# A split operand 64 bytes further, modulo 512, from the matrix it is mixed with

## The reference

```python
x = layernorm(x + attention(x))      # 16 heads, 4 key/value heads, old keys pooled in blocks of 64
x = layernorm(x + ffn(x))

def ffn(x):                          # x: [4096, 512]
    x = fwht(x * SU_ug) / 64         # Walsh-Hadamard transform over 512
    up   = x @ W_up.T   * (Wscale_ug[:2048] * 64)
    gate = x @ W_gate.T * (Wscale_ug[2048:] * 64)
    x = silu(gate) * up              # [4096, 2048]
    x = fwht(x * SU_dp) / 64         # over 2048
    return x @ W_down.T * (Wscale_dp * 64)
```

## Time and profile before

| | us |
|---|---|
| median of three runs | 1549.19 (1547.73 to 1554.15) |
| the profiled execution | 1548.87 |
| its span in the profile | 1547.1 |
| TensorE busy | 1513.5 |
| VectorE busy | 1034.0 |
| ScalarE busy | 625.8 |
| GpSimd busy | 465.0 |

### The profile page before, as it was taken

The page is one execution under the profiler, slowest core; times in us unless marked ns, Lnnn a source line. Parts: engine busy times, 40 slices in busy tenths (PEclk is TensorE's granted clock), DMA queues, the critical chain, the costliest instruction groups (busy, mean ns, idle before and its releaser), DMA issues.

```text
span 1547.1 us, 29636 instructions
## 1 busy us (share of the span) xinstructions
PE 1513.5 (98%) x11744; PEld 1422.1 (92%) x11744; DVE 1034.0 (67%) x1790; ACT 625.8 (40%) x1289; POOL 465.0 (30%) x580
## 2 busy tenths in 40 slices
PE   6999999999999999999999999999999999999998
PEld 5977978888887899899999999999999999999998
DVE  6876787677687886865575576566467547557645
ACT  4263245236227755533333343343343333334332
POOL 5465457438338533500220030030040022003001
PEclk9999999999999999999999999999999999999999
DMA  7031122122112796678578667767776857866862
GB/s 284 1 116 69 35 83 102 35 82 103 64 64 101 275 378 246 236 273 307 205 242 295 231 241 263 268 216 264 272 238 226 322 195 257 288 231 231 283 234 97
DMA packets 92072, 307.63 MB, mean 199 GB/s; under 512 B 9888, under 2 KB 10272, under 8 KB 90144
## 3 DMA queue, kind: packets, MB, share of 16 engines
q1 hardware_dynamic: 90928, 301.54, 54.8%
q10 hardware_dynamic: 1008, 4.20, 0.7%
HBM read 255.37 MB, written 50.33 MB: 198 GB/s over the span
## 4 chain that ended last, share of the span: by engine, by line
PE 64%; DVE 4%; ACT 1%; issue 1%; POOL 1%; POOLq 0%; DVEq 0%; ACTq 0%
PE ff_bank_b L2061 16%; PE ff_bank_a L2061 11%; PE ff_bank_c L2061 11%; PE ff_acc L2095 8%; PE ff_acc L2098 7%; PE ff_acc L2086 7%; DVE ff_d_lo L1775 2%; PE ff_x_ps L2020 1%; PE ff_x_ps L2009 1%; PE ff_x_ps L2032 1%; ACT at_union L601 1%; DVE ff_c L1826 0%; DVE ff_h_lo L1794 0%; DVE ff_c L1822 0%; DVE ff_ring L1770 0%
## 5 line engine op out<-in xcount | busy, mean ns | idle before, releaser
L2061 PE MATMUL ff_bank_b<-ff_x_hi,ff_ring 128*128 128x256 f32 x1536 | 296.8, 278 | 4.1 <-DVE ff_c L1826 3.5
L2061 PEld LDWEIGHTS ff_bank_b<-ff_x_hi,ff_ring 128*128 128x128 f32 x1536 | 246.3, 188 | 5.6 <-issue 5.4
L2061 PE MATMUL ff_bank_b<-ff_x_lo,ff_ring 128*128 128x256 f32 x768 | 212.8, 277 | 0.0
L2095 PE MATMUL ff_acc<-ff_d_lo,ff_h_hi 128*128 128x256 f32 x1008 | 199.8, 279 | 2.4 <-DVE ff_d_lo L1775 2.4
L2061 PE MATMUL ff_bank_c<-ff_x_hi,ff_ring 128*128 128x256 f32 x1024 | 200.3, 280 | 0.0
L2061 PE MATMUL ff_bank_a<-ff_x_hi,ff_ring 128*128 128x256 f32 x1024 | 199.6, 279 | 0.0
L2098 PE MATMUL ff_acc<-ff_d_hi,ff_h_lo 128*128 128x256 f32 x1008 | 197.7, 277 | 0.0
L2061 PEld LDWEIGHTS ff_bank_c<-ff_x_hi,ff_ring 128*128 128x128 f32 x1024 | 164.2, 188 | 2.2 <-issue 2.2
L2061 PEld LDWEIGHTS ff_bank_a<-ff_x_hi,ff_ring 128*128 128x128 f32 x1024 | 164.3, 188 | 0.3 <-issue 0.2
L1822 DVE TENSOR_TENSOR ff_c<-ff_bank_b,ff_c 128x512 f32<-128x512 f32 x64 | 44.3, 692 | 172.0 <-PE ff_bank_b L2061 171.1
L2095 PEld LDWEIGHTS ff_acc<-ff_d_lo,ff_h_hi 128*128 128x128 f32 x1008 | 152.9, 188 | 6.4 <-issue 6.4
(11 more groups left out here) (321 smaller groups left out, 3482.3 us busy)
## 6 DMA issues: line engine op xcount, KB each, us to landing
ff_ring<-gu_scratch SPq DMA_DIRECT2D x392, 512.0 KB, 5.1
gu_scratch<-ff_ring SPq DMA_DIRECT2D x56, 512.0 KB, 4.3
at_xt<-in_xt SPq DMA_DIRECT2D x4, 2048.0 KB, 8.0
at_xn<-in_x SPq DMA_DIRECT2D x32, 256.0 KB, 2.9
x_scratch<-at_x SPq DMA_DIRECT2D x32, 256.0 KB, 2.0
ff_raw<-in_wgu SPq DMA_DIRECT2D x8, 1024.0 KB, 7.1
at_wd_a<-in_wd SPq DMA_DIRECT2D x8, 512.0 KB, 4.0
mixed_scratch<-at_wd_a SPq DMA_DIRECT2D x8, 512.0 KB, 3.3
```

What stands on the lines that cost most here:

```text
L2061: i = pe.matmul(bank[:, m, :], r[:, a, m, c, :], b[:, k, c, :], start=(k < 3 and m == 0 and c == 0 and b is x_hi and a == 0), stop=(m == 1 ...
L2095: pe.matmul(acc[:, t, half], h_hi[q][:, j, k], d_lo[:, j, half], start=False, stop=False, skip_group_check=True)
```

## The change

`gap_behind` grows by 16 floats, which is 64 bytes per partition, and a tile of 112 floats (448 bytes) is put behind the two split tiles. `xs_hi` and `xs_lo` then stand at 64 modulo 512; everything behind them moves by 512 bytes. No instruction changes but for these addresses.

```diff
         sb("gap_in_front", [P, 16])
         d_hi, d_lo = sb("d_hi", [P, 2, D], F32R), sb("d_lo", [P, 2, D], F32R)
         x_hi, x_lo = sb("x_hi", [P, MULS, 2, HB2], F32R), sb("x_lo", [P, MULS, 2, HB2], F32R)
-        sb("gap_behind", [P, 1008])
+        sb("gap_behind", [P, 1024])
         xs_hi, xs_lo = sb("xs_hi", [P, FB], F32R), sb("xs_lo", [P, FB], F32R)
+        sb("gap_after", [P, 112])
         xm = sb("xm", [P, 8, FB])
```

## The result

The changed kernel takes 1568.73 us, the median of four runs (1567.53 to 1570.90). The kernel before took 1551.67 in its four (1547.73 to 1554.52). The ratio is 1.0113, with a 95% interval of 1.0083 to 1.0143. The profiled execution of after is 1569.43, its span 1567.6. The ratios are taken from the single executions and are not the quotients of the medians, from which they differ by up to 0.0022. One execution of the kernel before, 1573.59 us at a granted clock of 0.947, is left out of every ratio and counts only in the median of 1554.90 of its session.

A forecast was written before the change was run, and what follows sets the result against it. TensorE's stream of 256-column matmuls, at two lasting paces, was taken as the bound. 1548.87 - 0.2 + 0.95 + 0.35 + 19.3 = 1569.3 us, 1569.5 against the median; range 1547.5 to 1572.

The forecast's parts named there:

- The mixing no longer restores: At every mixing (L2020): at offset 64 it leaves the pace as it finds it, always slow; groups behind stay 1.41 us.
- The mixing itself: The 112 mixing matmuls: each between 113.3 and 120.8 ns instead of about 118.5; -0.6 to +0.3 us, taken as -0.2.
- Stretches behind a mixing: Stretches made fast by a mixing turn slow: 0.95 us over six blocks, 0.35 us in the first two blocks.
- The wait gives back 0.48 us: Block-end wait on VectorE's eviction: absorbs the slower 108 matmuls ahead of it, cost 0; otherwise 2.9 us in all.
- The restarts come out slow: Behind the six block-end waits: entered slow, the stream stays slow; 14.3 us for five blocks, 5.0 behind the sixth.
- four slow restarts: First block of the earlier trace: four of five different restarts came out slow, taken as evidence for slow late restarts.
- rival of fast restarts: Block-end waits entered slow come out fast, the instant being set by VectorE and GpSimd: 1550.0 us, chance 0.27.
- the offset does nothing: Something else in the mixing switches the pace, so it goes on as before: 1549 us, chance 0.11.
- The mixture: Two to four blocks restart slow by chance of the instant: 1556 to 1562 us, chance 0.15.
- it restores always: Every mixing at the new offset restores the fast pace, making the kernel faster: 1543.7 us, chance 0.05.

The follow-up runs named there:

- hi_only: Kernel before with only xs_hi at 64 bytes modulo 512, xs_lo staying at 0, the rest as in the changed kernel: 1567.30 us, ratio 1.0102.
- lo_only: Kernel before with only xs_lo at 64 bytes modulo 512, xs_hi staying at 0: 1565.53 us, ratio 1.0091.
- late_m7: Changed kernel with a 64-column VectorE memset ahead of the eviction L1827 in the last pair of every block but the first: 1563.01 us, ratio 1.0037.
- turn_64: Kernel before with the transposes' identity matrix 64 instead of 288 bytes modulo 512 from the y tiles: 1566.77 us, ratio 1.0078.
- same_shift: Kernel before with both splits still at 0 modulo 512 and all tiles from them on 512 bytes further: 1551.45 us, ratio 1.0009.
- last_at_0: Changed kernel with each block's fourth mixing back at 0 modulo 512, the other three at 64: 1565.46 us, ratio 1.0063.
- m7_first: Kernel before with VectorE's down-weight split put behind the eviction L1826 in the last pair of every block but the first: 1562.42 us, ratio 1.0048.
- all_448_m7: Kernel before with stream and splits at 448 modulo 512 and VectorE's late down-weight split behind the block-end eviction, first block excepted: 1562.94 us, ratio 1.0073.

## Why the prediction was right

The forecast was 1569.5 us and the measured median 1568.73. The closeness has luck in it. The sum starts from a profile of before in which all six restarts are fast and whose time, 1548.87, lies under every session's median (1550.78 to 1558.06). Against before in its own session the change costs 17.1 us by the medians, where the sum had 20.4.

**The mixing no longer restores: shown.** In the changed kernel all 28 are entered at 1.41 and leave 1.41. With one of the four back at 0 that one restores in five blocks of six and the others never do; with either half at 0 none does. That a mixing at 64 leaves the pace "as it finds it" is shown from the slow side only, since no run has one entered fast; at 448 both sides were seen.

**The mixing itself, -0.2 us.** Four matmuls take 0.47 us in after, 0.47 to 0.49 before. By the starts of the records the 28 mixings take 13.36 us in before and 13.19 in after, -0.18. The prediction's own figures (118.5 to 117.7 ns, 112 times) give only -0.09, so the -0.2 was a good guess.

**Stretches behind a mixing, 0.95 and 0.35.** Up to the first late restart the loss is 0.53 us, where 0.35 and a sixth of 0.95 - 0.2 were expected, 0.48. Here the agreement has luck in it: in the first block after restarted fast at 539.85 and before slow at 539.87, so those restarts differ between executions. Also, by the records, before has 56 matmuls made fast by a mixing in the first block, 0.25 us; the 36 of the second block are already among the six of the other term.

**The wait gives back 0.48 us: right.** The wait was 0.58, about 0.1 was to be left, and the chain of after shows 0.10 to 0.12. VectorE still ends the wait. In the third block its eviction ends at 904.66 in before and at 908.17 in after, and the restart follows 0.14 and 0.15 us later. It is on the chain in before and not in after only because TensorE's last matmul now ends later still, at 908.22.

**The restarts come out slow, 14.3 and 5.0: right in every one.** Five blocks cost 15.05 us where 14.3 + 5/6 of 0.75 = 14.9 was predicted, and the last 5.01 us against 5.0. This step had the weakest reason behind it, four restarts of the first block, and it decided. What the runs say of it is more, but does not settle it. Over all kernels with 64 bytes in the stream and a wait at the block's end, 28 restarts were entered slow: six each in the changed kernel, hi_only, lo_only and late_m7, two in turn_64, one each in same_shift and last_at_0. All 28 came out slow. Another 20 were entered fast: six in before, five in same_shift, four in turn_64, five in last_at_0. Of these 12 came out fast. By the starts of the single records these 12 have 854 to 855 ns from the last matmul ahead of the wait to the first behind it, and the eight slow ones 841 to 843. So "entered slow, comes out slow" held at every block's end; "entered fast, comes out fast", which the earlier trace rows suggested, held only with one length of the pause.

Whether the entry pace is the cause is not shown, since at the blocks' ends the entry pace and the length of the pause always came together: the 28 entered slow have 377 to 418 ns there, the 20 entered fast 841 to 855. The first block has pauses of other lengths, and there a stream entered slow came out fast three times: after 813 ns in the changed kernel itself (539.85), after 946 in same_shift and after 945 in last_at_0. In lo_only it came out slow after 940. Chain of waits of same_shift, then of lo_only:

```profile
516.84 1.41 PE ff_bank_a L2061 x12
...
518.92 1.60 PE ff_bank_b L2061 x12
520.52 1.36 PE ff_bank_c L2061 x12
```

```profile
516.33 1.41 PE ff_bank_a L2064 x12
...
518.40 1.65 PE ff_bank_b L2064 x12
520.06 1.41 PE ff_bank_c L2064 x12
```

Both are entered at 1.41, with pauses that differ by 6 ns. So the prediction's four slow restarts were not a rule, and its rival of fast restarts, which rested on the instant, had something to it: it failed because none of the six instants at the blocks' ends gave a fast restart.

**The rivals.** That the offset does nothing is out by same_shift and the changed kernel. The mixture is out for the changed kernel's profile, with six slow restarts of six, and its four times lie within 3.4 us. For the kernel before it may well be so in other executions: same_shift, of the same residues, has one slow restart in its profile. That it restores always is out: no mixing at 64 in a 64-byte stream restored.

**What stays open.** Why there are two paces, and what in the transposes picks one, no run shows. turn_64 says that their distance from the identity is not all of it. Why the two kernels differ in which mixing at 0 restores (m7_first, same_shift's second block) is not shown either. Why half of a mixing at 0 restores nothing is open as well. That the outcome goes with the length of the pause was seen in 20 cases entered fast, but never set on purpose: late_m7 tried, and its profiled execution shows no fast one.

Only the stream at 448 was faster than before, by 0.46%, and in one session only.

## What to carry to other kernels

When equal groups of matmuls in a chain of waits have two lengths, look for what stands where the length changes, and ask of an edit there not what it costs but what pace it leaves behind: four matmuls of 0.47 us decided over 648. A short wait in such a stream is also the place where the pace is drawn anew. Taking it away can freeze the worse one, as in m7_first and all_448_m7. And a tuned placement can look good by the chance of its pauses: in these runs 12 ns went with the difference between a fast and a slow restart.

## What the hardware showed beyond this

- The time between equal float32 matmuls depends on the distance modulo 512 between weights and moving data: 113.3 or 117.7 ns at 64 and at 448 bytes, 118.2 to 120.0 ns at 128. Between these kernels only the place of the moving data was changed. At 0 no stream was run; the last down has 119.6 to 120.0 ns by the starts of its records (the 120.8 of the prediction is the chain's 1.45 us over twelve).
- At 64 and 448 the two paces last: over 648 matmuls and more, until another kind of matmul or a wait stands between.
- One kernel of this kind spreads by itself. At a granted clock of 0.996 or more the kernel before ran at 1546.4 to 1564.4 us over all sessions, some 18 us. The pace of one block is 2.9 of them, and the attention part spreads too: in the profiles of all these kernels the second product of the feed-forward part starts at 517.4 to 521.5 us. That it is the pace that differs between these executions is not shown, since only one of them was profiled.
